# Moving the last gate's logits into products made earlier, from gate weights centred over the features

## The reference

```
x = x + gnn0(layernorm(x))     # x@w_self.T + segment_sum(w * x[src])@w_neigh.T, rows normed
x = x + ffn0(layernorm(x))     # shared MLP + top 2 of 4 small experts
x = x + gnn1(layernorm(x))     # relu([xn, mean of edge_attr by src, u] @ W1 + b1) @ W2 + b2
xn = layernorm(x)              # the "last" norm
scores = xn @ Wg.T + bg        # the last gate's logits: 8 experts
w, e = softmax(top2(scores))
x = x + sum of w * (relu(xn @ W1[e].T + b1[e]) @ W2[e].T + b2[e])
```

## Time and profile before

| | us |
|---|---|
| three timed runs | 3199.73, 3211.49, 3220.13 (median 3211.49) |
| span of the profiled execution | 4237.5 |
| of it: gathers, before 1,264 | 1264 |
| scatters, 1,264 to 2,357 | 1093 |
| rest of the first dense part, to 2,864 | 507 |
| edge sums, to 3,200 | 336 |
| last dense part, to 3,453.5 | 253.5 |
| experts | 784 |

### The profile page before, as it was taken

The page is one execution under the profiler, slowest core; times in us unless marked ns, Lnnn a source line. Parts: engine busy times, 40 slices in busy tenths (PEclk is TensorE's granted clock), DMA queues, the critical chain, the costliest instruction groups (busy, mean ns, idle before and its releaser), DMA issues. The chain is left out here.

```text
span 4237.5 us, 48325 instructions
## 1 busy us (share of the span) xinstructions
PE 2615.1 (62%) x11859; PEld 2002.8 (47%) x11860; DVE 1421.8 (34%) x3597; ACT 974.8 (23%) x2337; POOL 1860.1 (44%) x1901
## 2 busy tenths in 40 slices
PE   0445545556554221111211699998999879999998
PEld 0333334434443010100100466657996567888898
DVE  5211225666621000000000244438995542222222
ACT  4555222222220000000000244430003421111122
POOL 4566665665665777777777100002000342222222
PEclk9767667676776555555555799999998889999999
DMA  6223333332232111111111000006553454444455
GB/s 187 80 87 91 88 87 97 87 89 80 85 85 62 52 45 51 52 52 62 42 51 42 24 18 18 35 18 172 146 146 116 162 153 110 111 117 116 106 148 148
DMA packets 217917, 372.80 MB, mean 88 GB/s; under 512 B 48901, under 2 KB 146542, under 8 KB 216815
## 3 DMA queue, kind: packets, MB, share of 16 engines
q0 software_dynamic: 82928, 157.51, 14.4%
q1 hardware_dynamic: 77100, 154.03, 11.1%
q10 hardware_dynamic: 57812, 60.35, 5.0%
HBM read 290.03 MB, written 81.71 MB: 88 GB/s over the span
## 5 line engine op out<-in xcount | busy, mean ns | idle before, releaser
L673 PE MATMUL psum<-arena 128*128 x1984 | 632.1, 481 | 514.1 <-issue 325.7
L343 POOL DMA_INDIRECT arena<-xn_rows,arena x784 | 749.7, 956 | 449.7 <-issue 241.9
L904 POOL DMA_INDIRECT sorted_edges<-arena x768 | 766.7, 998 | 284.3 <-issue 265.1
L673 PEld LDWEIGHTS psum<-arena 128*128 128x128 f32 x1984 | 463.3, 243 | 683.1 <-issue 605.6
L408 ACT ACTIVATE arena<-arena 128x256 f32<-128x256 f32 x784 | 338.1, 496 | 697.3 <-DMA arena<-xn_rows,arena 642.6
L1177 PE MATMUL psum<-arena,acc 128*65 128x128 f32 x2720 | 311.9, 275 | 23.8 <-DVE arena L1330 23.8
L1177 PEld LDWEIGHTS psum<-arena,acc 128*65 128x65 f32 x2720 | 296.0, 138 | 40.1 <-DVE arena L1330 32.0
L1103 PE MATMUL psum<-arena 128*128 128x512 f32 (+1 forms) x336 | 172.3, 669 | 229.4 <-ACT arena L957 133.2
L1796 PE MATMUL psum<-arena,xr 128*128 x1344 | 301.7, 382 | 13.7 <-DVE xr L2021 9.1
L1783 PE MATMUL psum<-xr 128*128 128x256 f32 x1344 | 299.1, 381 | 1.0 <-DVE xr L2015 1.0
L575 DVE TENSOR_TENSOR acc<-acc,psum 128x256 f32 x248 | 103.0, 415 | 550.4 <-remote 366.8
(11 more groups left out here) (310 smaller groups left out, 3180.9 us busy)
## 6 DMA issues: line engine op xcount, KB each, us to landing
xr<-in_f_W_dram SPq DMA_DIRECT2D x63, 1024.0 KB
acc<-sorted_edges ACTq DMA_DIRECT2D x340, 132.0 KB, 2.2
arena<-in_attr_dram SPq DMA_DIRECT2D x28, 924.0 KB
arena<-xn_rows,arena POOLq DMA_INDIRECT x784
sorted_edges<-arena POOLq DMA_INDIRECT x784
arena<-hidden_parts SPq DMA_DIRECT2D x7, 1792.0 KB, 7.3
arena<-dispatched SPq DMA_DIRECT2D x42, 265.0 KB
arena<-in_f_W_dram SPq DMA_DIRECT2D x8, 1024.0 KB
```

The costliest lines, as they stand in the source:

```text
L343: pool.indirect_dma_start(out=rows[:, c, :], out_offset=None, in_=xn_d, in_offset=bass.IndirectOffsetOnAxis(ap=idx[:, c:c + 1], axis=0)).t ...
L673: last = nc.tensor.matmul(psum[:, bank(u), 0:D], hot[:, u, c, :], rows[:, ds(slots[k] + c, 1), :].squeeze(1), start=c == 0, stop=c == RUN - 1)
L904: pool.indirect_dma_start(out=edges_d, out_offset=bass.IndirectOffsetOnAxis(ap=pos_i[:, c:c + 1], axis=0), in_=stage[:, q % 2, c % SC, :], ...
```

## The change

In words, in order of time:

- `fg` is loaded ahead of the first dense part (one more of SP's first loads) instead of after it. PE sums its columns by the matrix of ones (2 products, `gate_sums`), DVE makes `fgc`, the centred weights.
- After each `part(c, g)` PE multiplies the same transposed rows `yT` by `fgc`: 8 products of 8 columns for c = 0, 6 for c = 1, after a wait for ACT's move of the third part product, whose bank they reuse. These rows are already normed by gnn1's norm, so DVE keeps that norm's deviation (a small copy in `first_rstd`; `rstd` is written with the deviation itself) and multiplies the products by it into `logit2` (`gate_rows2`, one instruction for each chain and group).
- After that part three more loads: the transpose of W2 in two pieces (256 KB each) and b2 by feature.
- At the start of the last dense part PE makes W2 C (8 products of 8 columns) and b2 C (2), DVE copies the first beside `gw2` and adds the second to `logit2`.
- `node(g, k)` is 264 columns wide instead of 256; DVE adds the eight extra columns to `logit2` (one small instruction for each tile).
- `turn`, `gate_columns` and `logits` are gone. `gates` has one instruction more. `gates`, `places` and the counts come one group earlier; the tables too; nothing of PE's is left after the last node product.

The diff, cut to its core:

```diff
@@ PE, first dense part, at the end of part(c, g) and before the loop
+                        if nth(c, g) == 0:
+                            pe.wait_ge(s_fgc, 1)
+                        pe.wait_ge(s_hc5, nth(c, g) * 4 + 3)
+                        for i, k in enumerate(CHAINS[c]):
+                            for j in range(2):
+                                last = nc.tensor.matmul(gate_part(c)[:, i * NX:(i + 1) * NX], yT[:, j, k * P:(k + 1) * P], fgc[:, j, :],
+                                                        start=j == 0, stop=j == 1)
+                        last.then_inc(s_lgp, 1)
+                    for j in range(2):
+                        last = nc.tensor.matmul(gate_sums, ones[:, :], fg[:, j, :], start=j == 0, stop=j == 1)
+                    last.then_inc(s_gsum, 1)
@@ PE, ffn(c, g), for m < 2
                                     pe.wait_ge(s_hc5, nth(c, g - 1) * 4 + 3 + m)
+                                    pe.wait_ge(s_lge, nth(c, g - 1) + 1)
@@ DVE, first dense part
                     def first_rstd(c, g):
                         dve.wait_ge(s_sd6, nth(c, g) + 1)
+                        own.add(nc.vector.tensor_copy(rstd[:, tiles(c, g)], ln["sd"][:, span(c)]))
                         rstd_of(c, s_ln6)
+                    def gate_rows2(c, g):
+                        dve.wait_ge(s_lgp, nth(c, g) + 1)
+                        nc.vector.tensor_tensor(logit2[:, tiles(c, g), :], gate_part(c).rearrange("p (k e) -> p k e", e=NX),
+                                                wide(rstd[:, tiles(c, g)], NX), ALU.mult).then_inc(s_lge, 1)
@@ PE, start of the last dense part
+                    for m in range(4):
+                        for c in range(2):
+                            last = nc.tensor.matmul(psum[:, 0, (m + 1) * NX:(m + 2) * NX], gw2T[:, 2 * c + m // 2, m % 2 * P:(m % 2 + 1) * P], fgc[:, c, :],
+                                                    start=c == 0, stop=c == 1)
+                    for c in range(2):
+                        last = nc.tensor.matmul(psum[:, 0, 5 * NX:6 * NX], gb2c[:, c:c + 1].to_broadcast([P, P]), fgc[:, c, :], start=c == 0, stop=c == 1)
                     last.then_inc(s_u5, 1)
@@ PE, node(g, k), and its loop
-                            last = nc.tensor.matmul(psum[:, 4 + k % 4, 0:D], h5[:, m, k * P:(k + 1) * P], gw2[:, m, :], start=m == 0, stop=m == 3)
+                            last = nc.tensor.matmul(psum[:, 4 + k % 4, 0:D + NX], h5[:, m, k * P:(k + 1) * P], gw2[:, m, :], start=m == 0, stop=m == 3)
                         for k in range(G):
-                            if k == 4 and g >= 2:
-                                counts(g - 2)
+                            if k == 4:
+                                counts(g - 1)
                             node(g, k)
-                            if k == 0 and g + 1 < NG:
-                                pe.wait_ge(s_tc5, PHASES * 2 + (g + 1) * 2 + 2)
-                            turn(g - 1, k)
-                            if k:
-                                logits(g - 1, k - 1)
-                        logits(g - 1, G - 1)
-                    for k in range(G):
-                        turn(NG - 1, k)
-                        if k:
-                            logits(NG - 1, k - 1)
-                        if k == 3:
-                            counts(NG - 2)
-                    logits(NG - 1, G - 1)
@@ ACT, loop of the last dense part
-                        if g >= 2:
-                            ratio(g - 2)
-                        gate_columns(g - 1)
+                        ratio(g - 1)
@@ DVE, last dense part
+                    nc.vector.tensor_copy(gw2[:, :, D:D + NX], psum[:, 0, NX:5 * NX].rearrange("p (m e) -> p m e", e=NX))
+                    nc.vector.tensor_tensor(logit2[:, :, :], logit2[:, :, :], psum[:, 0, 5 * NX:6 * NX].unsqueeze(1).to_broadcast([P, NT, NX]),
+                                            ALU.add).then_inc(s_gl6, 1)
                             dve.wait_ge(s_o5, g * G + k + 1)
+                            own.add(nc.vector.tensor_tensor(gt5["g"][:, k, :], psum[:, 4 + k % 4, D:D + NX], logit2[:, g * G + k, :], ALU.add))
                     def gates(g):
-                        dve.wait_ge(s_lg6, g + 1)
-                        nc.vector.tensor_tensor(gt5["g"][:, :, :], psum[:, 7 if g == NG - 1 else 2, 0:NX * G].rearrange("p (k e) -> p k e", e=NX),
-                                                fbg[:, :].unsqueeze(1).to_broadcast([P, G, NX]), ALU.add).then_inc(s_gl6, 1)
+                        own.add(nc.vector.tensor_tensor(gt5["g"][:, :, :], gt5["g"][:, :, :], wide(ln6["rstd"][:, :], NX), ALU.mult))
+                        own.sync()
+                        own.add(nc.vector.tensor_tensor(gt5["g"][:, :, :], gt5["g"][:, :, :], fbg[:, :].unsqueeze(1).to_broadcast([P, G, NX]), ALU.add))
-                        if g == EARLY + 2:
+                        if g == EARLY + 1:
                             first_table()
-                        if g >= 2:
-                            gates(g - 2)
+                        gates(g - 1)
                         node_sums(g, range(4))
-                        if g >= 2:
-                            places(g - 2)
+                        places(g - 1)
                         node_sums(g, range(4, G))
                     deviations(NG - 1)
-                    gates(NG - 2)
-                    places(NG - 2)
```

More of the change, by code:

```diff
@@ L700, in build @@
         spare = flat[:, NB * P:NB * D]
-        ph3 = Room(arena, early.at, ARENA)
+        gate_room = Room(arena, ARENA - (NT + 2) * NX, ARENA)
+        logit2 = sb("logit2", [P, NT, NX], f32, gate_room)
+        fgc = sb("fgc", [P, 2, NX], f32, gate_room)
+        ph3 = Room(arena, NC + 2 * SC * ER, ARENA - (NT + 2) * NX)
         if True:
@@ L1633, in _ @@
                     gate_rows(NG - 1)
-                    ratio(NG - 2)
-                    gate_columns(NG - 1)
                     act.wait_ge(s_w7, 16 * (NX + 2))
```

83 lines of the change are left out of this document (42 added, 41 removed).

## The result

| | us |
|---|---|
| before, median | 3214.27 (3199.73 to 3220.13, 4 runs) |
| changed, median | 3180.81 (3177.91 to 3188.31, 4 runs) |
| ratio | 0.9906, 95% interval 0.9881 to 0.9932 |
| the same again, run e11 | 3175.09 against 3206.57, ratio 0.9903 (0.9885 to 0.9922) |
| predicted | 3186, 3150 to 3235 |

The change takes 33 us, just under 1%, and both intervals agree. The forecast time was 5 us off, inside its own narrower range of 3,171 to 3,199; the forecast difference was 25 us for the measured 33.

The account below looks back on a forecast made before the run. POOL was taken to set stages 1 and 2, hiding the first dense part. Start +5, groups -21.6, late handoffs +5 and end -14 sum to -25.6, so -25 on 3,211: 3,186 us, range 3,150 to 3,235.

Parts of the forecast that it names:

- What bounds the kernel: In timed runs POOL sets stages 1 and 2; the first dense part has about 190 us of slack.
- late handoffs: Slow PE-to-ACT passes, 10.5 us where the work is 3.8, only where POOL issues indirect DMAs; +5 charged.
- the cover: POOL's scatters hide the work added to the first dense part: price 0; without it +25 to +35 us.
- rival (b): First dense part is on the path in timed runs as in the profile: +30, so 3,216; chance 0.15.
- The start: Ten more 8-column products ahead of everything in the last dense part: +5 us, bounds 2.6 and 6.
- A steady group: Last dense part, groups 2, 3 and 4: 17.3 us from last addition to reciprocal, -5.1 us each.
- then DVE sets the end: In a steady group DVE's gates, sums and places end behind PE; last sum and statistics end at 16.0 us.
- Rival (a): PE's full time in the last dense part comes back: 59 us less, 3,152; chance 0.15.
- Group 4: One of the three steady groups of the last dense part, forecast at -5.1 us.
- The end: Last node sum to first expert product, 22.6 us before, takes 7 to 8.5: -14, bounds -10 and -16.
- (c): PE runs the last dense part's node products at half clock: 54 us more, 3,240; chance 0.06.
- (d): Late handoffs and the first dense part on the path: +70 to +140 under the scatters, 3,250 and more; chance 0.06.

Follow-up runs that it names:

- e11: The changed kernel measured once more, with no edit: 3175.09 us, ratio 0.9903 to the kernel before.
- e1: The kernel before, unchanged, profiled a second time: profile span 3214.0 us.
- e2: Changed kernel with the added 8-column products of the first dense part made five times instead of once: 3182.93 us.
- e3: Changed kernel with the added 8-column products of the first dense part made thirteen times instead of once: 3518.58 us.
- e7: Changed kernel with one number changed, the second segment of scattered columns reaching to 704 and not 672: 3164.36 us.
- e4: Changed kernel with two unused transposes and two 8-column products given to PE after each node product of groups 1 to 6: 3196.94 us.
- e5: Changed kernel with DVE's small addition of the eight extra columns made twice for each tile: 3183.14 us.
- e8: Changed kernel with the start's products moved earlier, segment border at 704, and first three hidden products each waiting for their own tile's sum: 3354.90 us.
- e9: Changed kernel with separate waits for the first three hidden products and ACT's normed rows written after relus and exponential: 3167.99 us.
- e10: Changed kernel with the edits of e9 and the segment border at 704 of e7: 3153.59 us, ratio 0.9832 to the kernel before.

## Why the prediction was right, and where it was not

**What bounds the kernel.** Right, and the step that mattered most: the account of a timed run from rows without late handoffs. e1 shows each of its marks within 18 us up to the last dense part (which is 35 shorter than the 253.5 of the earlier trace rows). The forecast had "about 190" us of slack before the change. The first dense part became 35 us longer (the edge sums' first start, 1721.4 to 1756.4), and e2 and e3 show 151 us left, so 186 before. Nothing of the 35 is in the time. They are the upper end of what the forecast had reckoned without the cover, +25 to +35, so rival (b), 3,216, fell by the cover and not by the price. One figure of that account was short: 75 us of edge sums behind the last scatter are 85 (e7), as 84 items and not 76 stand there, before and after.

**The start.** 4.65 us measured on the path to the first `reciprocals`, against 4.6 + 0.7 less 0.3. Missed: the 12.31 us of `hidden(0)` behind them are no fixed cost. It takes 6.28 to 12.31 us in profiles of the same program by the moment at which the clock rises, so what the start costs net can't be told from one pair of profiles.

**A steady group.** -5.4 and -5.3 measured for -5.1, from parts that were not all right. PE's 0.57 x 7 = 4 us, which the step from node product to node product gave, is what e4 measured as 4.1. But "then DVE sets the end" is wrong: the ring over ACT's normed rows, relus and PE's node products does, with PE's own stream 0.9 us behind it (e4, e5, e8, e9). Three rows of e1's group 2, beside its reciprocal at 2317.54:

```profile
2296.73 2.00 PE L1718 MATMUL psum<-arena 128*128 128x256 f32 x8 [0.23 <-ACT arena L1599]
2313.25 0.42 DVE L1870 TENSOR_TENSOR xr<-psum,xr 128x256 f32<-128x256 f32 x1 [1.64 <-PE psum L1718]
2313.75 2.14 ACT L1593 ACTIVATE arena<-ident,rcount 128x128 f32<-128x128 f32 x7
```

From the first node product to DVE's first instruction on the last one are 16.5 us in e1 and 13.3 in the changed kernel, 3.3 less by the missing turns and logits. From there to the reciprocal are 4.3 in e1 and 2.1 in the changed kernel, 2.2 less: in e1 ACT makes seven spread reciprocals (2.14) and loads the square root's table (1.28) only behind the last turned tile. Both terms were in the forecast. Its 17.3 us from last addition to reciprocal were 0.8 too long (16.5 measured). Its own figures had the seventh node product done at 15.0, and DVE through with places and sums at 12.4 + 3 x 0.95 = 15.3, so the 16.0 that it went on with is PE's 15.0 and the last sum: the number followed PE where the sentence named DVE. PE is there at 14.4: the node products begin 1.15 us behind the last addition and not at once, but the first takes 2.1 and not 3.58 us, as the clock is 1.00. Rival (a), PE's full time back, was priced by busy time, 49.6 us; had it been priced by steps it would have been 0.6 x 49 = 29, and with the end and the start 29 + 14 - 5 = 38: 3,173, no other case than the forecast.

**The late handoffs.** +5 was charged, 0 came. In the changed kernel's steady groups POOL scatters beside `add_parts`, and the eight additions follow each other in 5.03 us, for 4.89 in e1's group 2 with no scatter beside them. The spans of all eleven profiles of the experiments, and that of the changed kernel, are within 13 us of the medians of their kernels' timed runs; the first profile of before alone is not. So "they stand only where POOL issues indirect DMAs" was a reading of one long execution, and no property of the kernel. What made that execution 1,026 us longer stays open; no run shows it again.

**Group 4.** -10.3 for -5.1: e1 has the clock at 0.59 there:

```profile
2341.00:2356.00 15.00, 14.87 (x26) 6.44 (x27) 7.61 (x23) 13.06 (x26) 9.94 (x11) 0.59 0.62 201
2341.67 10.36 PE L1704 MATMUL psum<-acc 64*128 64x512 f32 x16
```

It is the same as in e11's long interval, in `hidden` too, so it belongs to neither kernel. About 5 of the 36 us between the two profiles come from it by chance. Others work the other way: the changed kernel's fifth interval has a fall of the clock as well (25.6 us, and 23.7 and 23.9 in e11 and e2, which have none there), and its start is 5 us longer than in e2, e7 and e10. That the 36 come so near to the timed 33 is in part luck; the timed medians, taken twice, are the measure.

**The end.** -10.6 for -14, near its bound of -10. The first product starts 7.34 us behind the end of the last sum, inside the forecast's 7 to 8.5, by two misses that cancel: the load is issued 0.3 us behind the sum and not 1.3, and PE's first transposition of it starts 5.05 us after the issue where 3.5 were taken; the DMA engines' share is 1.00 in that stretch. What was too large is the 22.6 us of before; e1 has 18.2, counted the same way (2428.35 to 2446.52), as the bound had allowed for. No experiment changed the end by itself; it is read from the rows of both kernels.

**Not seen at all.** The experts are 2.4 us longer. The first expert products come after 5.86 us of idle PE and take 9.51 us for 32 records against 8.63 in e1, with a clock of 0.53 and 0.70 in their first 5 us, and behind the next wait of 2 us a stretch is slow once more (7.99 against 6.31). Nine of the ten later profiles that have the changed end take 769.4 to 770.5 us for the experts as well, but e3's takes 767.5, with no slow second stretch. So the 2.4 us are usual here and not a fixed price, and for the kernel before there is one such profile only.

**The other rivals.** (c), node products at half clock: out, they run at 1.86 us and a clock of 1.00. The Trainium skill (TensorE: Matmul & The Clock Gate, Part 1) has half rate as the default from which activity releases PE; the trace agrees at the start of the last dense part (0.50 in the first 7.4 us, 1.00 later) and at the experts (0.53, then 1.00). The falls while PE was busy (0.75 in e3, 0.66 in e11) don't follow from that sentence. (d), a slower kernel by late handoffs: out, there were none.

By the size of the terms in this one pair of profiles: +1.5 for +5, -30.3 for -16.6, -10.6 for -14, +3.1 for 0. The sum of the profiles is -36 and of the timed runs -33 for a forecast of -25. The mechanism held: the first dense part is hidden, each group is shorter by PE's turns and by the wait for the square root, and the end is shorter. The sum was 8 us short. 5 of them are the charge for late handoffs, an effect that didn't come; the rest is within what single terms move by chance.

## What to carry to other kernels

Price a removed or added PE instruction by the step from one neighbour to the next in a stretch with it and in one without, never by the sum of its records: here 0.6 and not 1.0 us a tile. Measure slack by putting in work of a known kind, in two sizes, before trusting or fearing a stage that looks long; it also shows where the path is, and here that pointed to a one-number edit worth another half of what the change brought. Before moving a consumer ahead, look in the queue for when its loads are issued, not for how long they take. And before a term of a few us is read from two profiles, take a second profile of the same kernel: here the start of one program took 33.4 to 41.2 us.

## What was new about the hardware

- PE's granted clock went down with the number of 8-column products though PE was busy for 99% of the time: 0.98 without them (e1), 0.95 with one copy of the new products, 0.85 with five, 0.75 with thirteen. A product, two records, then cost 0.39 and 0.42 us for an expected 0.26; the starts of its records stand 0.11 us apart at the high clock and 0.21 at the low one (e3).
- The same sixteen `hidden(0)` records behind the same fourteen products took 6.28, 9.7 or 12.31 us in nine profiles, by the moment at which the clock rose.
- In the profiles of e1, e5 and e11 a stretch of some 15 us in interval 4 has the clock at 0.59, 0.66 and 0.66 with PE busy, and the interval is 5 us longer. Every other profile of the changed groups but e2's has a fall in interval 5 or 6 (e5 a second one), some of them with PE partly idle; those that can be set against an interval without one (the changed kernel, e3 to e8) are 1.5 to 5.3 us longer. Why the clock falls there is open.
